# Turning an image attention's exponentials by DMA transposes instead of by TensorE

## The reference

```python
xn  = layer_norm(layer_norm(x))          # 4 x 512 x 128; ctx is normed too
q   = xn @ Wq * 64 ** -0.5               # 16 heads of 64
k,v = split(concat(xn, ctxn) @ Wkv)      # 666 keys
out = softmax(q @ k.T) @ v               # for each of 4 x 16 heads
x   = x + tanh(g_xattn) * (out @ Wo)
```

## Time and profile before

| | |
|---|---|
| median of 3 runs | 1660.23 us (1658.74 to 1662.96) |
| the profiled execution | 1667.16 us, its span 1665.3 us |
| PE busy over the span | 87% |
| DVE, ACT, POOL busy | 67%, 47%, 53% |
| mean granted clock of TensorE | 0.937 of full |
| hardware DMA queue | 59.83 MB, 12.2% of 16 engines' span |

### The profile page before, as it was taken

The page is one execution under the profiler, slowest core; times in us unless marked ns, Lnnn a source line. Parts: engine busy times, 40 slices in busy tenths (PEclk is TensorE's granted clock), DMA queues, the critical chain, the costliest instruction groups (busy, mean ns, idle before and its releaser), DMA issues.

```text
span 1665.3 us, 36883 instructions
## 1 busy us (share of the span) xinstructions
PE 1445.0 (87%) x13680; PEld 985.4 (59%) x13849; DVE 1110.9 (67%) x2918; ACT 780.5 (47%) x1566; POOL 877.9 (53%) x1308
## 2 busy tenths in 40 slices
PE   5999999999999897977888889979977777789987
PEld 3777777777777775755566555534544344434545
DVE  5889788878777773544764667854446567487753
ACT  4777667767766661632233355554234434211111
POOL 5789889978776693363335653422033332153330
PEclk8999999999999999998899899999987979789998
DMA  7333232111221111250000000000000000000000
GB/s 279 103 90 86 86 97 50 49 44 45 61 49 44 52 51 57 58 182 1 1 1 1 9 9 1 2 1 1 1 1 1 0 1 1 1 1 1 7 7 14
DMA packets 35479, 64.31 MB, mean 39 GB/s; under 512 B 7535, under 2 KB 25042, under 8 KB 34147
## 3 DMA queue, kind: packets, MB, share of 16 engines
q1 hardware_dynamic: 33831, 59.83, 12.2%
q0 software_dynamic: 1472, 2.12, 0.4%
HBM read 30.64 MB, written 12.66 MB: 26 GB/s over the span
## 4 chain that ended last, share of the span: by engine, by line
PE 35%; DVE 10%; ACT 4%; POOL 3%; issue 2%; DVEq 0%; ACTq 0%; POOLq 0%
PE banks L520 9%; PE banks L2210 3%; PE banks L2196 2%; PE banks L3058 2%; PE banks L3001 1%; PE banks L2723 1%; PE banks L2717 1%; PE banks L2163 1%; PE banks L495 1%; DVE work L2293 1%; PE banks L2199 1%; PE banks L1763 1%; PE banks L305 1%; PE banks L2985 1%; PE banks L1687 1%
## 5 line engine op out<-in xcount | busy, mean ns | idle before, releaser
L1059 POOL TENSOR_TENSOR work<-work 128x512 bf16<-128x512 f32 (+1 forms) x512 | 358.7, 723 | 76.4 <-ACT work L952 75.5
L835 DVE TENSOR_REDUCE work<-banks 128x1 f32<-128x666 f32 x256 | 216.4, 846 | 64.9 <-PE banks L752 62.2
L959 ACT ACTIVATE work<-banks,work 128x666 f32<-128x666 f32 x256 | 208.1, 813 | 30.3 <-DVE work L835 23.3
L952 ACT ACTIVATE work<-banks 128x512 f32<-128x512 f32 x256 | 152.8, 597 | 146.0 <-PE banks L763 145.7
L460 POOL TENSOR_TENSOR norm_room<-norm_room,minus_half 128x4 f32<-128x4 f32 (+1 forms) x56 | 53.1, 949 | 294.7 <-DVE norm_room L435 170.0
L763 PE MATMUL banks<-const,work 128*128 128x128 f32 x1024 | 159.2, 278 | 15.5 <-ACT work L952 12.3
L752 PE MATMUL banks<-work 128*128 128x154 bf16 (+1 forms) x898 | 160.4, 295 | 9.7 <-DVE work L909 1.6
L520 PE MATMUL banks<-work,weights_b 128*128 128x512 bf16 (+1 forms) x830 | 150.1, 337 | 13.6 <-ACT work L1348 7.0
L752 PEld LDWEIGHTS banks<-work 128*128 128x128 bf16 x1024 | 96.0, 98 | 80.6 <-DMA work<-work 2.8
L2293 DVE TENSOR_REDUCE work<-banks 128x2 f32<-128x308 f32 x192 | 87.0, 472 | 82.0 <-PE banks L2163 56.2
L791 PE MATMUL banks<-work 128*128 128x65 bf16 (+1 forms) x3840 | 136.6, 192 | 3.0 <-POOL work L1059 1.8
(11 more groups left out here) (463 smaller groups left out, 3294.7 us busy)
## 6 DMA issues: line engine op xcount, KB each, us to landing
work<-work SPq DMA_DIRECT2D x128, 166.5 KB, 2.8
sorted<-in_pads SPq DMA_DIRECT2D x10, 838.5 KB
weights_b<-in_weights SPq DMA_DIRECT2D x1, 4120.0 KB, 13.4
work<-scratch SPq DMA_DIRECT2D x64, 64.0 KB, 1.9
weights_b<-in_weights SPq DMA_DIRECT2D x1, 2824.0 KB, 12.3
weights_a<-in_weights SPq DMA_DIRECT2D x1, 2056.0 KB
weights_a<-in_weights SPq DMA_DIRECT2D x1, 2050.0 KB, 9.9
work<-work SPq DMA_DIRECT2D x32, 64.0 KB, 1.9
```

The costliest lines, as they stand in the source:

```text
L835: ve.tensor_reduce(self.neg_max[i % 4], self.slot[i % 2][:, 0:KEYS0], AX_X, ALU.max, negate=True).then_inc(self.mark("max"))
L952: ac.activation(self.probs_t[u % 2][:, h, 0:4, j * P:(j + 1) * P], self.bank_a.rearrange("p (t n) -> p t n", t=4), ACT.Copy).then_inc(self ...
L959: ac.activation(self.probs[i % 3], self.slot[i % 2][:, 0:KEYS0], ACT.Exp, bias=self.neg_max[i % 4]).then_inc(self.mark("exp"))
L1059: po.tensor_tensor(parts[:, :, :, 0], exact, parts[:, :, :, 1], ALU.subtract).then_inc(self.mark(event, i - 3))
```

## The change

The exponentials are no longer turned by TensorE.

- POOL splits the words before they are turned: one subtraction of 128x666 in place, so that each float32 word holds a high and a low bfloat16.
- SP turns the buffer by one DMA transpose per block. It reads 128 rows of 704 words (666 and zeros) as 1408 two-byte elements and writes 11 tiles of 128x128. A tile's 128 rows are 64 keys with two halves each, low and high in turn.
- So the values are laid out to fit: row 2k and row 2k + 1 of a tile both hold the value row of key k. ACT and DVE write plain rows (`v_rows`), and SP spreads them by six DMAs a group (`image_heads_sp`, case 2). The 154 context rows are projected as two tiles, 128 and 26; `four_times_po` and `ctx_last` go.
- Weighing is 11 tiles by two matmuls a block, by the values' high and low half (65 and 64 columns). The product low by low is now contained.
- TensorE's turns L763, L772, L775, ACT's copy L952, DVE's copies L843, L850, L851 and POOL's gathering L1065 go. Only the divided result is still turned by TensorE.
- `probs` has four buffers instead of three; the turned tiles have six (`TURNS`). The exponential of step i waits for the transpose of block i - 4. The transpose of block s waits for the weighing of block s - 6 to free its buffer.
- SP walks through the steps too: transposes, head copies, value copies and padding go through its one queue.

```diff
+        self.probs = [self.place(WORDS0 * HALF_KEYS) for _ in range(4)]
+        self.probs_t = [self.place(WORDS0, P, dt=BF16) for _ in range(TURNS - 2)]
 # image_weigh_pe
-            for t in range(KT0 - 1):
-                for which, (of_values, of_probs, width) in enumerate(orders):
-                    pe.matmul(self.out_heads[:, 2 * j + h, 0:width], parts[:, h, t, j * P:(j + 1) * P, of_probs], v[:, t, of_values, h, 0:width],
+            sub = 4 * u + 2 * h + j
+            pe.wait_ge(*self.turned_in(sub))
+            for t in range(WORDS0):
+                for part, width in ((0, D0 + 1), (1, D0)):
+                    m = pe.matmul(self.out_heads[:, 2 * j + h, 0:width], self.probs_t[sub % TURNS][:, t, :], v[:, t, part, h, 0:width],
 # image_ac
-                if i >= 3:
-                    ac.wait_ge(*self.at("turned_b", i - 1))
-                    ac.wait_ge(*self.at("gathered", i - 3))
+                if i >= 4:
+                    ac.wait_ge(*self.turned_in(i - 4))
                 ac.wait_ge(*self.at("max", i + 1))
 # image_po
             if 1 <= i < SUBS + 1:
+                whole = self.probs[(i - 1) % 4][:, 0:KEYS0]
                 po.wait_ge(*self.at("exp", i))
+                po.tensor_tensor(self.halves(whole)[:, :, 0], whole, self.halves(whole)[:, :, 1], ALU.subtract).then_inc(self.mark("low_a", i - 1))
 # image_sp
+        for i in self.image_steps():
+            n = (i - 1) // 8 + 1
+            if i % 8 in (1, 5, 7) and n < GROUPS0:
+                self.image_heads_sp(sp, n, (1, 5, 7).index(i % 8))
+                if i % 8 == 5 and 2 <= n < 2 + PAD_PARTS:
+                    self.pads_sp(sp, n - 2)
+            if 1 <= i < SUBS + 1:
+                sub = i - 1
+                if sub >= TURNS:
+                    sp.wait_ge(*self.at("weighed", (sub - TURNS) // 2 + 1))
+                sp.wait_ge(*self.at("low_a", sub))
+                sp.dma_start_transpose(self.probs_t[sub % TURNS], self.probs[sub % 4].bitcast(BF16)).then_inc(...)
 # image_heads_sp, case 2
+            sp.wait_ge(*self.at("v_low", 3 * n + 3))
+            if n >= 3:
+                sp.wait_ge(*self.at("weighed", 2 * (2 * n - 4)))
+            for word in (0, 1):
+                for h, own in ((0, top), (1, bottom)):
+                    sp.dma_start(v[word::2, h:WORDS0 - 1:2, :, :], rows[own, 0:KT0 - 1, :, :])
+                sp.dma_start(v[word:2 * CTX_REST:2, WORDS0 - 1, :, :], rows[0:CTX_REST, KT0 - 1, :, :])
```

More of the change, by code:

```diff
@@ L39 @@
 KT0 = -(-KEYS0 // P)
+HALF_KEYS = P // 2
+WORDS0 = -(-KEYS0 // HALF_KEYS)
+TURNS = 6
 EXPERTS, FF = 8, 512
@@ L225, in step @@
         return self
-    wait_ge = then_inc = dma_start = matmul = transpose = activation = memset = reciprocal = bn_stats = bn_aggr = step
+    wait_ge = then_inc = dma_start = dma_start_transpose = matmul = transpose = activation = memset = reciprocal = bn_stats = bn_aggr = step
     indirect_dma_start = reg_load = tensor_copy = tensor_tensor = tensor_scalar = tensor_reduce = scalar_tensor_tensor = tensor_tensor_reduce = step
@@ L753, in image_scores_pe @@
         m.then_inc(self.mark("scores"))
[L755 to L776, removed]
@@ new lines, in image_turn_pe, with turned_in, values_in @@
+    def image_turn_pe(self, pe, u):
+        ps = self.bank(pe, 5, "mixed", u + 1)
+        pe.wait_ge(*self.at("divided", u + 1))
+        for j in (0, 1):
+            m = pe.transpose(ps[:, j * P:(j + 1) * P], self.divided[:, 2 * j:2 * j + 2, :].rearrange("p h d -> p (h d)"), self.eye)
+        m.then_inc(self.mark("mix_turned"))
+    def turned_in(self, sub):
+        return self.at(f"dma_turn{sub % TURNS}", 16 * (sub // TURNS + 1))
+    def values_in(self, n):
+        return self.at("dma_values", 96 * (n + 1))
@@ L837, in image_ve @@
                 self.image_lows_ve(ve, (i - 1) // 8 + 1, (i - 1) % 8 // 2)
[L838 to L847, removed]
-                    ve.wait_ge(*self.at("weighed", u - 1))
-                ve.wait_ge(*self.at("turned_b", i))
-                ve.wait_ge(*self.own("ve", ve.tensor_copy(whole, self.bank_b[:, P:2 * P])))
-                ve.tensor_tensor(self.halves(whole)[:, :, 0], self.bank_b[:, P:2 * P], self.halves(whole)[:, :, 1],
-                                 ALU.subtract).then_inc(self.mark("low_c", u))
             u = self.mix_due(i)
@@ L1103, in image_sp, with image_heads_sp @@
         self.loads(sp)
+        for which in range(3):
+            self.image_heads_sp(sp, 0, which)
+        self.load_weights(sp, 1)
+        for i in self.image_steps():
[9 more added lines that the diff above has]
+                sp.wait_ge(*self.at("low_a", sub))
+                sp.dma_start_transpose(self.probs_t[sub % TURNS], self.probs[sub % 4].bitcast(BF16)).then_inc(self.mark(f"dma_turn{sub % TURNS}", n=16), 16)
+    def image_heads_sp(self, sp, n, which):
         top, bottom = slice(0, D0), slice(D0, 2 * D0)
-        for n in range(GROUPS0):
-            q, k, low = self.q[n % 2], self.k[n % 2], self.q_part
+        q, k, low, v, rows = self.q[n % 2], self.k[n % 2], self.q_part, self.v[n % 3], self.v_rows
+        if which == 0:
             sp.wait_ge(*self.at("q_low", n + 1))
```

137 lines of the change are left out of this document (43 added, 94 removed).

## The result

The changed kernel takes 1901.41 us, the median of 4 runs (1897.39 to 1905.76), beside 1659.49 us for the kernel before in the same sessions: a ratio of 1.1465, 95% interval 1.1414 to 1.1516. The forecast was 1967 us in a range of 1600 to 2450.

A forecast was written before the change was run, and what follows sets the result against it. TensorE bounded the old step of 2.35 us; SP's queue would bound the new: 8 x 2.3 + 10.0 = 28.4 us a group, 3.55 a step, +307 us, so 1967 us, range 1600 to 2450.

The forecast's parts named there:

- The place and the sign: Image attention: SP's queue becomes the limit, so the kernel gets slower, by 307 us; chance of slower 0.78.
- TensorE's relief: Image attention: TensorE's step falls to 1.77 us, a gain of 148 us if the DMAs cost nothing.
- The issue of a turn: SP's queue: issuing one transpose takes 2.3 us, the geometric middle of 0.60 and 8.81.
- The rest of the queue: SP's queue: copies of 7.5 us and a wait of 2.5 us, 10.0 us a group without the turns.
- The wait behind the first query copy: SP's queue: waiting for that copy to land behind a turn takes 2.5 us a group, today 0.8.
- The engines: The 16 DMA engines: 2.2 us a step, 1.7 to 2.8 at the ends, inside the queue's step; share about 0.6.
- the forecast's mechanism: SP's queue: issuing the turns sets the step at 3.55 us; 1790 to 2200 us, chance 0.61.
- Rival 2: DMA engines, not the queue, are slow at turning: 8.5 us a turn, 3390 us, middle case 2260 us; chance 0.17.
- Rival 1: SP's queue and DMA engines: turns cost about what straight copies do, giving 1550 to 1622 us; chance 0.18.
- the break-even: SP's queue: the change gains only if one turn's issue is below 1.1 us.

The follow-up runs named there:

- m3: Changed kernel's SP queue alone, all computation left out: 24.1 us a group quiet, 25.0 us beside busy compute engines.
- m1: No computation, only turns of 11, 6 or 1 tiles and plain copies from SP's queue: a lone 11-tile turn issues in 1.40 us.
- e1: Changed kernel with the six value copies of a group issued from ACT's queue instead of SP's: 1921.18 us, ratio 1.1571.
- e3: Changed kernel with each turn from the seventh on taking 6 of 11 tiles, the rest left stale: 1789.09 us, ratio 1.0786.
- m2: No computation, only value copies, key copies and turns from SP's queue: a set of value copies every 4.4 us, turns with keys and values 21.3 us a group.
- e7: Changed kernel with eight turned and two value buffers, values copied for two groups only, one-tile turns from the ninth on: 1652.90 us, ratio 0.9957.
- e9: Changed kernel with two buffers for the doubled values instead of three, six turned buffers kept: 1860.67 us, ratio 1.1250.

## Why the prediction held, and where its numbers were off

**The place and the sign** held. The time went into SP's queue and its DMAs, and TensorE's relief could not pay for them. The changed kernel's trace shows it: the queue hardly ever stands still for an engine that computes. m3 agrees: the queue alone takes about the kernel's group.

**The issue of a turn** was the term chosen between 0.60 and 8.81 us as 2.3, 26 ns for each of 88 blocks. It is 1.40 us alone (m1), nearly all of it fixed. In the kernel after the padding it is 1.6 us in the median and 1.71 in the mean, stretched by the full engines. Eight of them are 13.7 us instead of 18.4. This term was mis-sized most, by 4.7 us a group, 150 us in all. The Trainium skill counts 32 cycles a tile (DMA: Bandwidth & Descriptors, in the table of the older descriptor generation), which the prediction took for each of the 88 blocks, an estimated 2.35 us. The runs don't bear this reading out: from 48 to 88 blocks the issue grew by 0.19 us. The table doesn't say how large its tile is.

**The rest of the queue** was taken at 10.0 us. The means after the padding give 1.8 for the queries, 2.7 for the keys and 4.5 for the values, 9.0 where 7.5 was priced. The wait behind the first query copy was 32.0 us over 27 groups, 1.2 each instead of 2.5. The pauses between issues, 0.05 us each and 1.2 a group, stood in no term. Sum: 13.7 + 9.0 + 1.2 + 1.2 = 25.1 us, measured 25.2 without padding, forecast 28.4. The padding, priced at nothing, added 3.4 us to each of ten groups, 34 us in all: 0.9 are its own issue, and in the same groups a turn takes 1.99 us in the mean for 1.71. So the forecast lay within 66 us partly by luck: the 150 us too many for the turns were in part made up by these terms, which were too small or missing.

**The engines** were put inside the queue's step, at 2.2 us of it and a share of 0.6. The share is 0.96. A turn costs them 1.7 us instead of 1.5, inside its bounds of 1.0 to 2.1, and a set of values 3.2 us instead of 1.9. The sum of the pieces measured alone (8 x 1.7 + 2.7 + 3.2, and the queries) is about 20 us, so the share in the kernel counts more than the work of each alone. What the rest is stays open. So the forecast's mechanism was half of the truth. Rival 2, slow engines, is the other half, at the low end of its price. What did not hold is the overlap: the forecast put the engines' work inside the queue's step, at a share of 0.6, with no effect on the issues. They fill the step, and they lengthen the issues. e1 shows that relieving the queue alone gains nothing, e3 that relieving the engines stops at the queue. One queue in order uses both badly: while it issues small copies the engines run at 0.73, and while it issues turns it waits for them. That last sentence is argued from m2's windows and not shown by a run that separates the two.

**Rival 1** fell on both sides. Turns do move as plain copies do, but only as copies of 256-byte runs: 210 GB/s in m1, not the 350 to 400 that the Trainium skill gives (Advanced Engine Details and Errata, X-Bar Transpose). And an issue costs 1.4 us, where 1.1 was the break-even.

**TensorE's relief** was put at 0.58 us a step, 148 us, if DMAs cost nothing. No run tests this, since none has turns without an issue. e7, the nearest, shows 2.20 us a step from 360 to 560 us, where the kernel before does 84 steps, 2.38 each, and 7 us in all. It is held mostly by its queue, 16.4 of 17.5 us a group. What TensorE alone would need stays open; its clock fell too (0.95 to 0.97 in e7, 0.87 in the changed kernel), and the forecast priced it at nothing.

**Small terms.** POOL's subtraction was forecast at 1.30 us and takes 1.304. TensorE is busy 128.8 of 200 us (300 to 500 us), more than the half forecast, at a clock of 0.86. The weighing was expected to wait for DMAs and does not; the exponential was, and does. No version here beats the kernel before without leaving work out. Two that might were not tried: turning half of the blocks by DMA and half by TensorE, and one DMA for the turns of two blocks.

## What to carry to other kernels

Price a DMA that replaces engine work three times: its issue on the queue, its time on the engines by its run length, and what it now stands behind in that queue. Here a turn of 352 KiB costs 1.4 us of issue with little regard to size, which speaks for few large ones (not tried), and it moves at the rate of 256-byte copies. A busy TensorE is worth relieving only down to the next limit. A kernel whose new DMAs move next to nothing (e7) shows what their number alone costs before the real ones are built. And read a queue's waits from the pauses between its issues: a view that infers them from semaphores named 66.1 us here where there were none.

## What was not expected of the hardware

- A turn's issue is almost independent of its size: alone 1.09 to 1.13 us for one tile, 1.21 for six, 1.37 to 1.40 for eleven (m1).
- Copies from a second queue stretched the first queue's issues, from 1.7 to 2.6 us a turn (e1).
- Moving the tiles by 5.8 KB in each partition, or having two value buffers for three, made a 256-byte packet shorter, 21.1 ns for 24.0, the median issue 0.2 us shorter and the kernel about 2% faster (1.1250 against 1.1465, e9). The cause is open.
- The turning itself costs the engines a little: in m1 a packet of 256 B takes 21.7 ns in the mean in the turns and 18.3 in the plain copy.
- TensorE's granted clock was 0.86 in the mean from 300 to 500 us, between its two levels of 1.2 and 2.4 GHz, with TensorE busy 128.8 of 200 us and waiting in between; in the kernel before it was 1.00 there, with 189.6 us busy.
